# Two residual row loads moved behind the reads of the reciprocals in SyncE's slot 6

## The reference, cut to what matters

```python
ln_out = layernorm(hidden_states, ln1_s, ln1_b)
q, k, v = jnp.split(ln_out @ w_qkv + b_qkv, 3, axis=-1)
x = hidden_states + merge_heads(attention(q, k, v, ltor_mask)) @ w_ao + b_ao
ln_out = layernorm(x, ln2_s, ln2_b)              # cross attention on encoder_states
x = x + merge_heads(attention(q, k, v, cross_mask)) @ w_co + b_co
x = x + gelu(layernorm(x, ln3_s, ln3_b) @ w1 + b1) @ w2 + b2
# then the non-local block: theta, phi, g, W = theta phi / n, y = W g, 1x1 conv, batch norm, + x
```

## Time and profile before

| | us |
|---|---|
| median of 3 runs | 2017.9 |
| lowest and highest of them | 2016.56, 2021.75 |
| the profiled execution, its own time | 2019.01 |
| its span, first to last instruction | 2017.2 |

### The profile page before, as it was taken

How to read it: one execution, slowest core, us unless ns; L and a number is a source line. 1 busy time by engine, 2 the same in 40 slices (tenths; PEclk the granted TensorE clock), 3 DMA queues, 4 the chain that set the end, 5 groups by cost and what they waited for, 6 DMA issues and landing times. The chain is left out here.

```text
span 2017.2 us, 41550 instructions
## 1 busy us (share of the span) xinstructions
PE 1980.1 (98%) x13632; PEld 1571.8 (78%) x13632; DVE 1470.2 (73%) x3868; ACT 1160.5 (58%) x3251; POOL 546.7 (27%) x556
## 2 busy tenths in 40 slices
PE   9999999999999999999999998999999999999998
PEld 9877777777777777777777776888888888888887
DVE  7799989998998998998899989564444343435333
ACT  4388788887888888888887888521212111212111
POOL 1012212222234343333334342054032231313000
PEclk9999999999999999999999999999999999999999
DMA  8446676576678877767777744531212213121201
GB/s 284 161 94 129 151 172 141 132 166 143 132 190 183 185 185 167 167 171 180 152 173 179 162 109 118 171 101 41 78 38 72 68 44 81 47 62 50 62 24 48
DMA packets 681720, 252.67 MB, mean 125 GB/s; under 512 B 533312, under 2 KB 626112, under 8 KB 681536
## 3 DMA queue, kind: packets, MB, share of 16 engines
q1 hardware_dynamic: 563264, 235.69, 45.3%
q10 hardware_dynamic: 118272, 14.69, 4.7%
HBM read 167.41 MB, written 82.84 MB: 124 GB/s over the span
## 5 line engine op out<-in xcount | busy, mean ns | idle before, releaser
L1331 ACT ACTIVATE A_p<-A_p,A_nmax 128x256 f32<-128x256 f32 x1024 | 507.2, 501 | 3.7 <-DVE A_res L1614 1.7
L1646 DVE CUSTOM_DVE_ANT_0 A_p<-A_p,A_ma 128x256 f32<-128x256 f32 x1024 | 374.6, 420 | 4.6
L1636 DVE TENSOR_TENSOR A_p<-A_sc,A_mk 128x1024 f32<-128x1024 f32 x256 | 312.2, 1220 | 52.7 <-PE A_tp L1093 52.0
L842 POOL TENSOR_TENSOR A_ct_l<-A_cx,A_ct_h 128x256 fp32r<-128x256 f32 x122 | 114.1, 935 | 679.6 <-DVE A_nmax L1646 666.1
L1348 ACT ACTIVATE A_pt<-A_tp 128x512 f32<-128x512 f32 x396 | 218.1, 587 | 49.1 <-PE A_tp L1093 47.6
L1093 PEld LDWEIGHTS A_tp<-A_ident,A_p 128*128 128x128 f32 x1584 | 179.9, 141 | 73.0 <-ACT A_p L1331 36.6
L1093 PE MATMUL A_tp<-A_ident,A_p 128*128 128x128 f32 x1584 | 223.6, 278 | 2.9 <-ACT A_pt L1348 2.1
L1485 ACT ACTIVATE A_mk<-A_tp,A_cols 128x512 f32<-128x512 f32 x62 | 42.7, 689 | 269.0 <-PE A_tp L68 269.0
L1331 ACT ACTIVATION_READ_ACCUMULATOR A_p<-A_p,A_nmax 128x1 f32 x1024 | 197.5, 193 | 0.0
L1485 ACT ACTIVATE A_ma<-A_tp,A_cols 128x512 f32<-128x512 f32 x62 | 42.8, 690 | 243.0 <-PE A_tp L68 243.0
L66 PE MATMUL A_banks<-A_xt_h,A_w_h 128*128 128x512 f32 x384 | 162.1, 422 | 8.8 <-DVE A_res L1614 8.3
(11 more groups left out here) (248 smaller groups left out, 4997.1 us busy)
## 6 DMA issues: line engine op xcount, KB each, us to landing
exponentials<-A_ln_shift SPq DMA_DIRECT2D x464, 64.0 KB, 2.4
A_pt<-exponentials SPq DMA_DIRECT2D x116, 256.0 KB, 4.2
A_x<-x SPq DMA_DIRECT2D x96, 256.0 KB, 3.9
A_res<-x SPq DMA_DIRECT2D x64, 256.0 KB, 3.2
A_rt<-inverses SPq DMA_DIRECT2D x512, 32.0 KB, 2.2
x<-A_res SPq DMA_DIRECT2D x64, 256.0 KB, 4.7
turned<-A_x ACTq DMA_DIRECT2D x224, 64.0 KB, 2.8
A_e<-ctx_t SPq DMA_DIRECT2D x16, 512.0 KB, 4.1
```

What stands on the lines that cost most here:

```text
L842: pool.tensor_tensor(ct_l[:, f, part], cx[:, :], f32(ct_h[:, f, part]), ALU.subtract).then_inc(c_lo, 1)
L1331: act.activation(p[:, g % 2, j, t, :], p[:, g % 2, j, t, :], ACT.Exp, scale=-1.0, bias=nmax[:, g % 2, j, t:t + 1], accum_out=rsum[:, g % 2 ...
L1636: dve.tensor_tensor(p[:, g % 2, heads, :, :].rearrange("p j t s -> p j (t s)"), sc[:, heads, :], m, ALU.mult)\
L1646: dve.tensor_tensor_reduce(out=a_, in0=a_, in1=ma[:, b, t, :], scale=-1.0, scalar=BIG, op0=ALU.add, op1=ALU.min, accum_out=nmax[:, g % 2, ...
```

## The change

In slot 6 of bodies 1 to 15 `load_res` of tiles 2 and 3 is issued after `store_exponentials` and `load_inverses`, and no longer before them. Nothing else is changed; the same DMAs are issued, with the same waits.

```diff
@@ -635,13 +635,13 @@
                     load_exponentials(r, h, pv)
                 if own:
                     store_inverses(r, h)
-                    if h == 6 and 0 < k < NU:
-                        for t in range(2):
-                            load_res(k - 1, r - 1, t + 2)
                 if exists(k, h, 0) and moved(group(r, h, 0)[0]):
                     store_exponentials(r, h)
                 if own:
                     load_inverses(r, h)
+                if h == 6 and 0 < k < NU:
+                    for t in range(2):
+                        load_res(k - 1, r - 1, t + 2)
                 if h == 0 and k > 1:
                     for t in range(2):
                         load_res(k - 1, r - 1, t)
```

## The result

The changed kernel takes 2027.2 us in the median of 5 runs (2023.8 to 2033.1), the kernel before 2018.5 beside it. The ratio is 1.0049 with a 95% interval of 1.0032 to 1.0066: slower by 7 to 13 us, about 10, outside my range of 2010.5 to 2025.5, and on the other side of no change. The profiled execution took 2023.8 us and is the fastest of the five; it is only 4.8 us above that of before, so the profile shows about half of the loss.

What follows compares the result with a forecast made beforehand. TensorE, busy 98% of the span, was taken as the bound, so only its waits could be won. 1.8 us gained after capping, less 0.3 lost on the queue, gave 1.5: 2017.9 to 2016.4 us, range 2010.5 to 2025.5.

Steps and rivals of the forecast that it cites:

- TensorE's wait for the sum of tile 3: First product of each new body waits until VectorE has added residual tile 3: 14 times, 8.3 us together.
- VectorE's gap in slot 7: VectorE's `scaled` waits for the reads of the reciprocals, once in each of bodies 1 to 14: 14.2 us, 13.3 removable.
- meeting: Slot 7: GpSimd's later bias addition of tile 2 overlaps VectorE's maxima; costs its length less 0.15, 10.9 us over fourteen bodies.
- The reads of the reciprocals come forward by 0.94 us only: Slot 6, body 10: the reads start at 858.0, not 858.94, because they wait for the store of the reciprocals to land.
- The slow rival: Reads of the reciprocals, right behind the four writes, take 5.1 us to land in every body: 11.5 us slower, 2029.4; chance 0.08.
- Tile 2 lands 2.9 us after its issue: Residual load moved behind the four reads in slot 6: body 10's tile 2 lands at 862.9.
- The lower end of the range: With residual loads landing after 4.3 us, the bias addition's loss is full, 15.8 us, and the capped sum -2.6.
- Behind the loads on the queue: Moved loads stand before the next read of the turned exponentials, which has 1.8 us slack: 0.3 us lost, bounds 0 to 3.
- The sum: Over the fourteen bodies: 1.8 us gained, 0.3 lost, so 1.5 us faster, 2016.4 us in the median.
- 0.02 of the chance for slower: Share of the 0.10 chance of a slower kernel given to loads that push the reads behind them on the queue.

## Why the prediction was wrong

By its own steps:

- *TensorE's wait for the sum of tile 3 is VectorE's gap in slot 7.* Right. With the gap nearly away and no meeting, it falls from 8.3 to 1.4 us and the kernel gains 9.7 us, where I had capped the gain at 8.0. The interval of that ratio, 7 to 12 us, holds both.
- *The reads of the reciprocals come forward by 0.94 us only, and the gap of slot 7 goes.* Right in kind: the reads still wait for the store's landing. In body 10 they start 4.2 us after the store's issue, 5.7 before, so they came forward by 1.4 us, since the store landed after 4.2 us and not 4.6. In bodies 1 to 14 the gap is 0, not 14.3 us, and in body 10 the reads take 3.5 us from their first issue to the last landing. The slow rival, reads that take 5.1 us, did not come about. Its price was also wrong in body 10: slower reads move the maxima back, away from the addition, so they don't by themselves bring a full meeting.
- *Tile 2 lands 2.9 us after its issue.* Right: 2.9 in the median.
- *The meeting costs its length less 0.15; 10.9 us over fourteen bodies.* The size was off by a quarter: 8.2 us by the trace, 8.3 by experiment. In body 10, where I forecast 0.64 us, it was 0.05. The lower end of the range was also misread: with a landing of 4.3 us the addition of body 10 would run from 864.35 to 865.63, mostly behind the maxima that end at 864.79, so the loss there would be small and not full.
- *Behind the loads on the queue: 0.3 us, 0 to 3.* This is the step that failed. It measured about 11 us. I asked whether the next read of the exponentials, in slot 7, still lands before TensorE needs it, found 1.8 us of slack, and stopped. For slot 7 that was nearly right: the read takes 5.6 us to land in the median, 4.5 before, and TensorE waits for it once, 1.3 us. I did not follow the store of the reciprocals of slot 7, which lands just behind that read. It lands later, SyncE stands at the reads that wait for it, and what stands behind them in SyncE's order (row loads, stores of the residual, the next read of the exponentials) is held back. In slots 0 and 1 the read of the exponentials landed 5.5 us after the slot's first product in the median of the bodies before, and the product with v began at 7.1: 1.6 us of slack. After the change the reads land at 6.9 and 7.3. The trace of before had these numbers.
- *The sum.* By the measured terms: 9.7 gained, 8.3 and 11.3 lost, 9.9 slower, which is the ratio of 1.0049. These terms are differences of ratios that add up to it by construction, so the sum proves nothing by itself. The profiles speak for it on their own: 8.2 us by which the maxima grew, and 9.9 us more of TensorE's waits for the exponentials.

I named this mechanism under the range, as 0.02 of the chance for slower, and gave the other side to a rival that did not happen. I had bounded the delay at 1.4 us for a single read. It came up again and again: TensorE waited five times in slot 0 and eight times in slot 1, and only one wait in each stood there before. The rule of the Trainium skill that I weighed last ("DMA: Bandwidth & Descriptors", section "Queues, rings and completion order"), that descriptors are consumed in ring order, gave the sign of it. The trace agrees: the read of slot 7 landed 1.1 us later in the median, with the two loads in front of it.

What stays open: the chain from slot 7 to slots 0 and 1 is read from the rows, and no run breaks it at the store alone. The bytes of the moved loads are needed for the loss, since without them nothing remains of it. But half of these bytes cost nothing measurable, and two narrow transfers that are added cost 7 us; why, no run here shows.

## What to carry to other kernels

In this kernel a queue that one engine issues in order, and whose small transfers that same engine waits for, had free places and dear ones. The free place was ahead of an issue that had to wait for a landing anyway (0.9952 and 0.9927); with four loads in it, too many for the wait, the time was 1.0017. Look for such places. When a transfer is moved, follow each small transfer behind it to the next two or three stages, not only the next large one. And ask what the data's later arrival makes run at the same time as what: here an addition on GpSimd, which is busy for 27% of the span, stopped VectorE.

## What the runs showed of the hardware

A GpSimd addition that arrives in the middle of the maxima also stops them. The rows of body 9 above show it: GpSimd's took 1.52 us in place of 1.29, so it seems to have waited for the running maximum, and the next one then lost 1.10 us. That is the case that no row of before had. By the Trainium skill, "SBUF — State Buffer", section "Who interferes with whom", it was to be so: the shared pair of ports is an exclusive lock, and the second to issue fully blocks. The trace agrees: the addition lost 0.23 us behind the maximum, and the next maximum 1.10 us behind the addition.

A store of the reciprocals, 16 KB, took between 1.4 and 6.1 us to land in the changed kernel (3.8 in the median, 3.6 before, from 190 to 1200 us). By slots, in the median of bodies 1 to 14: 1.4 us in slots 4 and 5, 4.3 in slot 0 and 5.0 in slot 1. In slots 7, 0 and 1 it landed 0.2 us (median) behind the 256 KB read of the exponentials that was issued before it, and in no body less than 0.16 us.
